# Decoder layers on one core: the last attention rows, the second half's spread, the expert weights' splits and the end of the mixture, rearranged

## What is computed

```
x = x + xattn_1(layernorm(x), ctx)     # 3 rounds: scores, softmax over the slots, weighted rows, GRU
x = x + ffn_1(layernorm(x))            # below

def expert_step(acc, w):
    wg, wu, wd = w                     # 128x512, 128x512, 512x128
    h = silu(x @ wg) * (x @ wu)
    return (acc + h @ wd, None)
acc, _ = scan(expert_step, zeros_like(x), (Wg, Wu, Wd))     # 8 experts
```

## Time and profile before

| | |
|---|---|
| three executions | 780.71, 776.95, 779.32 us, median 779.32 |
| profiled execution | 777.27 us |
| its span, first to last instruction | 775.5 us |
| TensorE | busy 673.7 us, 87% of the span |
| VectorE, ScalarE, GpSimd | 76%, 68%, 58% |
| mean granted TensorE clock | 0.946 |
| the mixture's units in that span | 649.1 to 771.3 us |

### The profile page before, as it was taken

How to read it: one execution, slowest core, us unless ns; L and a number is a source line. 1 busy time by engine, 2 the same in 40 slices (tenths; PEclk the granted TensorE clock), 3 DMA queues, 4 the chain that set the end, 5 groups by cost and what they waited for, 6 DMA issues and landing times.

```text
span 775.5 us, 23846 instructions
## 1 busy us (share of the span) xinstructions
PE 673.7 (87%) x8894; PEld 484.3 (62%) x8894; DVE 586.3 (76%) x1100; ACT 529.0 (68%) x1153; POOL 450.0 (58%) x486
## 2 busy tenths in 40 slices
PE   5789999999999999997743868899888788899997
PEld 2257776777777777775521467788877676444443
DVE  5878888887777777889788566888888887755663
ACT  3267777767677777775473398999999884455554
POOL 1666777777777777781100033667776973466664
PEclk9799999999999999999985978989999889999999
DMA  6535444444444444331400602640644441002100
GB/s 191 153 88 174 133 127 118 122 135 139 139 139 130 133 128 132 94 103 19 168 28 0 246 2 84 239 175 10 241 167 165 167 165 43 0 2 81 42 0 25
DMA packets 26721, 86.16 MB, mean 111 GB/s; under 512 B 5829, under 2 KB 7493, under 8 KB 26645
## 3 DMA queue, kind: packets, MB, share of 16 engines
q1 hardware_dynamic: 26264, 84.73, 34.4%
q10 hardware_dynamic: 384, 0.46, 0.2%
HBM read 65.19 MB, written 0.46 MB: 85 GB/s over the span
## 4 chain that ended last, share of the span: by engine, by line
PE 49%; DVE 15%; ACT 14%; POOL 10%; issue 8%; SPq 2%; DMA 1%; POOLq 0%; DVEq 0%; ACTq 0%
PE ps L1493 10%; POOL ctx_lo L675 9%; PE ps L1510 8%; PE ps L1524 8%; ACT c_prob L840 7%; PE ps L1480 4%; PE ps L1751 3%; PE ps L1469 3%; DVE tile_max L935 3%; PE ps L1733 2%; ACT w0T L840 2%; PE ps L1529 2%; ACT merge_w L840 2%; DVE amax_part L1151 1%; SPq L510 1%
## 5 line engine op out<-in xcount | busy, mean ns | idle before, releaser
L935 DVE TENSOR_REDUCE tile_max<-ps 128x1 f32<-128x500 f32 x336 | 214.6, 675 | 49.5 <-PE ps L1493 48.9
L701 ACT ACTIVATE probs<-ps 125x896 f32<-125x896 f32 x192 | 175.3, 916 | 92.8 <-PE ps L1510 92.0
L1493 PE MATMUL ps<-k_hi,qdiag 128*128 128x500 f16 x336 | 129.8, 389 | 6.2 <-DVE tile_max L935 3.2
L840 ACT ACTIVATE c_prob<-ps,c_bias,row_scale 125x56 f32<-125x56 f32 x384 | 118.8, 547 | 7.9 <-DVE c_bias L1239 7.9
L1510 PE MATMUL ps<-qstack,kstack 98*125 98x224 f16 x768 | 106.7, 262 | 0.4
L630 POOL TENSOR_TENSOR c_prob<-c_prob,c_weight 125x672 f32<-125x672 f32 x32 | 43.1, 1347 | 101.9 <-DVE c_weight L1253 101.7
L675 POOL TENSOR_TENSOR ctx_lo<-ctx_hi,ctx_lo 128x448 f16<-128x448 f32 x64 | 70.2, 1098 | 53.3 <-ACT ctx_lo L876 53.3
L1510 PEld LDWEIGHTS ps<-qstack,kstack 98*125 98x125 f16 x768 | 86.3, 137 | 21.1 <-ACT probs L701 2.8
L1733 PE MATMUL ps<-query_hi,ctx_hi 128*128 128x56 f16 x576 | 54.8, 193 | 28.8 <-ACT c_prob L840 20.8
L1524 PE MATMUL ps<-probs,v_aug 125*32 125x168 f32 x1536 | 74.8, 312 | 3.3 <-ACT probs L701 2.5
L572 POOL TENSOR_TENSOR qstack<-q_rep,slot_mask 96x224 f16<-96x224 f32 (+1 forms) x64 | 33.7, 556 | 75.3 <-PE ps L1510 70.3
(11 more groups left out here) (278 smaller groups left out, 1707.2 us busy)
## 6 DMA issues: line engine op xcount, KB each, us to landing
row_tiles<-in_ctx_rows_wide SPq DMA_DIRECT2D x40, 774.0 KB, 5.7
ctx<-in_ctxT SPq DMA_DIRECT2D x16, 750.0 KB, 5.2
rows_in<-in_ctx_rows SPq DMA_DIRECT2D x16, 750.0 KB
kstack<-k_hi SPq DMA_DIRECT2D x128, 93.8 KB, 2.8
kstack<-k_lo SPq DMA_DIRECT2D x64, 93.8 KB, 2.7
ctx_hi<-in_wg SPq DMA_DIRECT2D x8, 256.0 KB, 2.7
ctx_hi<-in_wu SPq DMA_DIRECT2D x8, 256.0 KB, 3.1
ctx_hi<-in_wd SPq DMA_DIRECT2D x8, 256.0 KB, 3.6
```

Of the source, the lines that this page charges most:

```text
L701: nc.scalar.activation(probs[c % RING_P][0:CH, :].rearrange("p (k w) -> p k w", k=2), score_tile(c)[0:CH], ACT.Exp, scale=float(HD) ** -0. ...
L840: last = nc.scalar.activation(c_prob[n % PROBS][:, c, :], ps[0:CH, 2 * (n % 2) + c // 6, bass.ts(c % 6, TOK)], ACT.Exp, bias=c_bias[n % 2] ...
L935: nc.vector.reduce_max(tile_max[:, u % MAXT, u // MAXT:u // MAXT + 1], ps[:, MAXB + (u + p) % 2, 0:KCOLS], AX.X).then_inc(max_done, 1)
L1493: nc.tensor.matmul(ps[:, MAXB + (u + p) % 2, 0:KCOLS], qdiag[p][:, bass.ts(t, 128)], k_hi[p][:, bass.ts(j, KCOLS)], start=True, stop=True) ...
```

## The change

- `update_rows(11)` is issued on VectorE inside `new_slots(10)`, ahead of its wait for the candidate's tanh, and no longer at slot 205.
- TensorE issues units 8 and 9 of the mixture ahead of `half_spread(1)`, and VectorE product 8 ahead of `half_norm(1)`.
- The weights of experts 3 to 7 are split in pieces of 512 columns, all on VectorE, one piece behind one product (highs behind the first three products of an expert, lows behind the next three); for expert 3 six pieces behind products 19, 20 and 21, two each.
- The low halves of the hidden values of units 62 and 63 are taken by VectorE, each right behind its own product, and not by GpSimd.
- Half 0 of the stream is finished when output 62 is there, half 1 when output 63 is, and each half is stored by a transfer of its own.

```diff
 def splits_until(e):
-    return 3 * min(e, SOON) + max(e - SOON, 0)
+    return 3 * e
...
-            sp.wait_ge(x4_done, 2)
-            sp.dma_start(out, xT[:]).then_inc(stored, 16)
-            sp.wait_ge(stored, 16)
+            for h in range(2):
+                sp.wait_ge(x4_done, h + 1)
+                sp.dma_start(out[:, bass.ts(h, HALF)], xT[:, bass.ts(h, HALF)]).then_inc(stored, 16)
+            sp.wait_ge(stored, 32)
...
-            for u in range(UNITS_F):
+            for u in range(UNITS_F - 2):
                 i = u % RING
                 pool.wait_ge(h_hi_done, u + 1)
...
             def new_slots(g):
                 slots = slots_of(g)
+                if g == GROUPS_C - 2:
+                    update_rows(g + 1)
                 dve.wait_ge(cand_done, g + 1)
...
+            def piece_high(m):
+                e, at = m // 3, bass.ts(m % 3, PIECE)
                 dve.wait_ge(h_used, units_until(e - 3))
                 dve.wait_ge(w1_loaded[e % 2], 48 * (e // 2 + 1))
-                nc.vector.tensor_scalar(w1_hi[e % 3], w1_f32[e % 2], W1_SCALE, None, ALU.mult).then_inc(w1_hi_done, 1)
+                nc.vector.tensor_scalar(w1_hi[e % 3][:, at], w1_f32[e % 2][:, at], W1_SCALE, None, ALU.mult).then_inc(w1_hi_done, 1)
...
+            def hidden_low(u):
+                i = u % RING
+                dve.wait_ge(h_hi_done, u + 1)
+                dve.wait_ge(h_lo_done, u)
+                nc.vector.tensor_tensor(hidden_lo[i], hidden[i], hidden_hi[i], ALU.subtract).then_inc(h_lo_done, 1)
+
+            def rows_in_turn(g):
+                if g < GROUPS_C - 1:
+                    update_rows(g)
...
                     hidden_of(7)
+                    hidden_of(8)
                     half_norm(1)
...
-            for u in range(8, UNITS_F):
+            for u in range(9, UNITS_F):
                 hidden_of(u)
                 if u == 19:
-                    weights_high(SOON)
+                    piece_high(3 * SOON)
+                    piece_high(3 * SOON + 1)
+                if u == 20:
+                    piece_high(3 * SOON + 2)
+                    piece_low(3 * SOON)
                 if u == 21:
-                    weights_low(SOON)
+                    piece_low(3 * SOON + 1)
+                    piece_low(3 * SOON + 2)
                 e, rest = divmod(u, 2 * F1)
-                if rest == 1 and SOON <= e < EXPERTS - 1:
-                    weights_high(e + 1)
-                if rest == 4 and SOON <= e < EXPERTS - 1:
-                    weights_low(e + 1)
+                if SOON <= e < EXPERTS - 1:
+                    if rest < 3:
+                        piece_high(3 * (e + 1) + rest)
+                    elif rest < 6:
+                        piece_low(3 * e + rest)
+                if u >= UNITS_F - 2:
+                    hidden_low(u)
             for h in range(2):
-                dve.wait_ge(h_used, UNITS_F)
+                dve.wait_ge(h_used, UNITS_F - 1 + h)
...
-                    expert_units(6, 8)
+                    expert_units(6, 10)
                     half_spread(1)
...
-            expert_units(8, UNITS_F + LAG)
+            expert_units(10, UNITS_F + LAG)
```

More of the change, by code:

```diff
@@ L1356, in half_norm, with piece_low @@
                 nc.vector.tensor_tensor(x_lo[:, at], stream[:, at], x_hi[:, at], ALU.subtract).then_inc(x_lo_done, 1)
-            def low_part(e, i, n):
-                at = slice(PIECE * i, PIECE * (i + n))
+            def piece_low(m):
+                e, at = m // 3, bass.ts(m % 3, PIECE)
+                dve.wait_ge(w1_hi_done, m + 1)
                 nc.vector.scalar_tensor_tensor(out=w1_lo[e % 3][:, at], in0=w1_f32[e % 2][:, at], scalar=W1_SCALE, in1=w1_hi[e % 3][:, at],
                                                op0=ALU.mult, op1=ALU.subtract).then_inc(w1_lo_done, 1)
[L1364 to L1368, removed]
+            def piece_high(m):
+                e, at = m // 3, bass.ts(m % 3, PIECE)
                 dve.wait_ge(h_used, units_until(e - 3))
                 dve.wait_ge(w1_loaded[e % 2], 48 * (e // 2 + 1))
-                nc.vector.tensor_scalar(w1_hi[e % 3], w1_f32[e % 2], W1_SCALE, None, ALU.mult).then_inc(w1_hi_done, 1)
-            def weights_low(e):
-                dve.wait_ge(w1_hi_done, splits_until(e + 1))
-                low_part(e, 0, 3)
+                nc.vector.tensor_scalar(w1_hi[e % 3][:, at], w1_f32[e % 2][:, at], W1_SCALE, None, ALU.mult).then_inc(w1_hi_done, 1)
             def hidden_of(u):
@@ L1416, in beside @@
                     hidden_of(7)
+                    hidden_of(8)
                     half_norm(1)
             iterations(unit, [
-                (VECTOR_AT["rows"], False, update_rows), (VECTOR_AT["scaled"], True, scaled_queries), (VECTOR_AT["hidden"], False, hidden_part),
+                (VECTOR_AT["rows"], False, rows_in_turn), (VECTOR_AT["scaled"], True, scaled_queries), (VECTOR_AT["hidden"], False, hidden_part),
                 (VECTOR_AT["slots"], False, new_slots), (VECTOR_AT["slots"], True, slot_squares), (VECTOR_AT["root"], True, root_guess),
                 (VECTOR_AT["lo"], True, query_low)], before_drain=lambda: weights(UNITS_C - 1), beside=beside)
-            for u in range(8, UNITS_F):
+            for u in range(9, UNITS_F):
                 hidden_of(u)
                 if u == 19:
-                    weights_high(SOON)
+                    piece_high(3 * SOON)
[3 more added lines that the diff above has]
+                    piece_low(3 * SOON)
                 if u == 21:
-                    weights_low(SOON)
+                    piece_low(3 * SOON + 1)
+                    piece_low(3 * SOON + 2)
                 e, rest = divmod(u, 2 * F1)
-                if rest == 1 and SOON <= e < EXPERTS - 1:
-                    weights_high(e + 1)
-                if rest == 4 and SOON <= e < EXPERTS - 1:
-                    weights_low(e + 1)
+                if SOON <= e < EXPERTS - 1:
[5 more added lines that the diff above has]
+                    hidden_low(u)
             for h in range(2):
-                dve.wait_ge(h_used, UNITS_F)
+                dve.wait_ge(h_used, UNITS_F - 1 + h)
                 nc.vector.scalar_tensor_tensor(out=xT[:, bass.ts(h, HALF)], in0=ps[:, 4 + h, 0:HALF], scalar=1.0 / W1_SCALE,
```

## The result

Eight executions of the changed kernel took 771.06 to 775.48 us, median 772.54; eight of the kernel before, on the same chip, 776.56 to 782.27, median 777.98. The ratio is 0.993, interval 0.9911 to 0.9948: 5.4 us faster by the medians, 4.0 to 6.9 by the interval. The profiled execution took 772.33 us, its span 770.5 us, against 777.27 and 775.5.

What follows compares the result with a forecast made beforehand. TensorE was taken as the bound in the mixture, so only its gaps can be won: 0.93 + 0.14 + 1.85 (weights) + 0.43 (end) = 3.35 us off the median 779.32 gives 776.0, range 772.0 to 780.0.

Steps and rivals of the forecast that it cites:

- rows divided first: Last group's division on VectorE, moved into idle time: TensorE's transposes and the chain behind come 0.93 us earlier.
- spread two units later: Half 1's spread behind unit 9: the 2.23 us gap goes, products 7 and 9 hold TensorE; 0.14 us gained.
- holds of experts 4 to 7: Four TensorE waits for VectorE products behind whole weight instructions: pieces remove them, 2.17 us won.
- hold ahead of unit 24: TensorE's wait for product 22 behind expert 3's six pieces: 0.95 us against 0.63 before, 0.3 us lost.
- end: additions and outputs: Last output 0.41 us later through VectorE's low halves, but half 1's single shorter addition ends sooner: 0.13 us gained.
- end: store: Final store of 224 KB lands in 2.2 us where 448 KB took 2.5: 0.3 us saved.
- both holds: TensorE waits in the drain: 1.14 us ahead of unit 9 for product 7, 0.95 ahead of unit 11 for product 9.
- free lateness of 0.75: In the mixture, a VectorE product may come 0.75 us late before TensorE loses time.
- (1): Rival: both drain holds stay away and expert 3's pieces cost nothing new; 4.8 to 6.4 us gained; chance 0.2.
- (2): Rival: gains cancel, slot update holds the gates' sums, expert 3's pieces hold by 1.3; 0.9 to 2.2 gained; chance 0.22.
- (3): Rival: GpSimd's next low half also passes each waiting piece in the mixture; 9.2 us slower, 788.5; chance 0.06.
- (4): Rival: the parts fall where TensorE is not held; within 0.5 us of no change, 779; chance 0.02.

Runs made afterwards that it cites:

- late-rows experiment: The changed kernel with the last rows divided at slot 205 again, behind group 10's slot update: stretch 122.6 us against 121.6, median of four 773.87 us.
- kernel with three places set anew: The changed kernel with VectorE's product 9 before the norm, product 7 inside half 1's root, product 63 before low 62: stretch 118.7 us against 121.6, median 767.8.

## Why the prediction was right, and where its sizes were off

The range and the sign held: forecast 776.0 in 772.0 to 780.0, measured 772.54, 0.5 us inside its lower end. The likeliest outcome did not come: 0.54 stood on "within 0.5%", and the ratio is 0.7% under one. Of the 3.4 us between forecast and median 1.3 are the base (the median of before was 779.32 in three executions and 777.98 in eight), 1.4 are the steps (forecast 3.35 us, 4.8 in the stretch), and the rest, 0.6, is what the medians (5.4 us apart) show beyond the stretch. The range held by the us added at its end for scatter and by a rival whose mechanism came only in part, so that it held is partly luck; that the mechanism was right is not. By its steps, against the traces of before and after:

| step | forecast | measured |
|---|---|---|
| rows divided first | 0.93 | 1.0 |
| spread two units later | 0.14 | 0.46 |
| holds of experts 4 to 7 | 2.17 | 2.17 (4 x 0.54, none left) |
| hold ahead of unit 24 | 0.63 to 0.95 | 0.63 to 0.24 |
| end: additions and outputs | 0.13 | 0.19 |
| end: store | 0.3 | 0.58 |

**The rows divided first**: right in place, in size and in what follows. The slot update ended in time (650.97, the gates' sums start at 651.39), and the late-rows experiment shows that no slack lies behind.

**The spread**: the mechanism was right, both holds came where they were put, which a reading of the gap alone would have missed. The sizes were 1.07 for 1.14 and 0.80 for 0.95, and the spread itself takes 0.88 us (669.73 to 670.61) where it was costed at 0.98; three small terms of one sign, 0.07, 0.15 and 0.10, make the difference of 0.32 us.

**The weights in pieces**: the waiting for GpSimd was costed rightly (1.27 us for a high piece, 1.54 for a low one; measured 1.25 to 1.28, and 1.52 for the first low piece of an expert but 1.25 for the next two, since GpSimd's row is 0.33 us further on when they start). The free lateness of 0.75 was right too: products came 0.03 to 0.3 us late with no hold, and product 22, 0.98 late, held TensorE by 0.24, which leaves 0.74. The mis-sized term is expert 3's: a hold of 0.95 was taken as the middle between 0.6 and 1.3. Product 22 was due at 688.65 + 3 x 1.703 = 693.76 and started 694.74, 0.98 late, where 1.3 was the lower end. I had added up the waits too pessimistically: two highs in a row took 1.61 us and put product 20 only 0.37 late, and between the two lows GpSimd did not slip in: the second low starts at about 694.14 (it ends at 694.82, and one takes 0.68), GpSimd's instruction 0.11 us later, and it waited itself (1.46 us in place of 1.03). That step is 0.7 us off, the largest error.

**The end**: low(62) did keep product 63 back, as forecast, 0.34 us for 0.41. Half 1's addition starts 0.78 behind the last output as before, and the stream is done 768.12 - 763.68 = 4.44 us behind the start of output 61, against 4.63. The store was mis-sized: 224 KB land in 1.9 us, under the 2.1 of 56 KB that I had taken as a floor. That floor was a transfer of another kind, within SBUF and of other rows, and was no bound.

The rivals: (1), bigger, is nearest to what came by its size (4.8 us) but only by half of its mechanism: expert 3's pieces cost nothing new, and both drain holds are there. (2) fell: the slot update did not hold the gates' sums. (3) fell: no piece was passed by a second low half at any of 24 places in experts 4 to 7 (GpSimd's rows there stay at 1.03 to 1.04 us). (4) fell.

## What to carry to other kernels

When one engine is busy without a break, a reordering is worth the holds of that engine which it removes, less those it makes: list each with who ends it, and ask of each moved instruction what is queued behind it on the helper's list. Here the moved spread gave back 1.9 of 2.2 us to two products that stood behind other work in a hand-written list, and placing three instructions anew won 2.9 us more. For parts under a microsecond, compare a stretch of the trace that begins at a fixed instruction, not whole times.

## What was not expected of the hardware

GpSimd's low halves, which read SBUF, cost the changed kernel 2.1 us, 1.84 of it in the drain, against a memset (0.47 us, reading nothing; which of the two differences does how much of it was not tried apart): half 1's add takes 1.34 us beside GpSimd's low half and 0.62 without it, a root step of 112 columns 1.10 and 0.28. So the two engines do not meet only at semaphores, as the text on the engines has it: each can make the other's instruction longer. A half-size store lands in 1.9 us where the whole takes 2.5, so that the split saves 0.58 us at the end of the span. And the part of the kernel ahead of the mixture, the same instructions each time, ended anywhere from 642.6 to 652.9 us; what moves it was not settled. The traces show one difference: in the earliest of them, the kernel with three places set anew, the mean granted clock of TensorE from 500 to 525 us was 1.00, and 0.86 to 0.93 in the other eleven. Which is cause and which effect is open.
